# Mamba stage of a five-layer model: products of the late tiles issued beside those of the early tiles, and a section's first wait lowered by one copy

## The reference

```
B = (x @ W_B.T).reshape(b, L, h, n)          # h = 16 heads, n = 64 states
C = (x @ W_C.T).reshape(b, L, h, n)
X = x_in.reshape(b, L, h, p) * dt[..., None] # p = 8
Y_diag = einsum('bclhn,bcshn,bhcls,bcshp->bclhp', C, B, Lmat, X)
states = einsum('bclhn,bhcl,bclhp->bchpn', B, decay_states, X)
...
y = Y.reshape(b, L, d) * silu(z)
y = y @ W_out.T
```

## Time and profile before

| what | value |
|---|---|
| runs, us | 712.9, 714.73, 713.87; median 713.87 |
| profiled execution, us | 712.9, of which span 710.9 |
| granted TensorE clock, mean | 0.993 |
| share of the span busy: TensorE matmul, weight load | 94%, 70% |
| VectorE, ScalarE, GpSimd | 80%, 59%, 45% |
| sections of the Mamba stage | first D at 431.79 us, last O at 593.68 us |
| one section in the loop (516.91 to 537.42 us), granted clock | 1.00 |

### The profile page before, as it was taken

One profiled execution on the slowest core, in us unless ns is written; L12 is line 12 of the kernel. 1 busy time (PEld: TensorE's weight loads), 2 busy tenths in 40 slices (PEclk: granted clock), 3 DMA queues, 4 the chain that ended last, 5 costly groups with the idle time before them and its releaser, 6 DMA issues. The chain is left out here.

```text
span 710.9 us, 12357 instructions
## 1 busy us (share of the span) xinstructions
PE 665.9 (94%) x4084; PEld 498.0 (70%) x4084; DVE 566.6 (80%) x1303; ACT 416.6 (59%) x755; POOL 322.6 (45%) x403
## 2 busy tenths in 40 slices
PE   7899998797899999999999978999999998999997
PEld 5677774543457777777777767777777775777785
DVE  5789978989987888888989877666766676879775
ACT  4557685986335555556556567555656555555554
POOL 2568874101227756646647725220413300545463
PEclk8999999999999999999999999999999999999999
DMA  6625430000005232222222100000000000423241
GB/s 171 204 91 190 134 117 1 0 1 0 2 7 158 75 105 90 53 98 76 97 68 79 57 1 1 2 2 2 1 2 0 0 1 2 120 75 119 57 123 45
DMA packets 34345, 43.16 MB, mean 61 GB/s; under 512 B 5232, under 2 KB 17520, under 8 KB 34288
## 3 DMA queue, kind: packets, MB, share of 16 engines
q1 hardware_dynamic: 34288, 42.46, 19.6%
HBM read 41.13 MB, written 1.31 MB: 60 GB/s over the span
## 5 line engine op out<-in xcount | busy, mean ns | idle before, releaser
L726 POOL TENSOR_TENSOR p_prod<-p_p,p_gate_row 128x512 f32<-128x512 f32 x128 | 202.7, 1595 | 106.6 <-DVE p_p L524 59.6
L399 ACT ACTIVATE p_sil<-p_ps_a 128x512 f32<-128x512 f32 x176 | 105.1, 597 | 130.8 <-PE p_ps_a L100 125.0
L529 DVE TENSOR_TENSOR p_hlo<-p_prod,p_hhi 128x512 fp32r<-128x512 f32 x176 | 149.5, 851 | 0.3 <-ACT p_hhi L408 0.2
L524 DVE TENSOR_TENSOR p_p<-p_sil,p_ps_b 128x512 f32<-128x512 f32 x128 | 87.0, 680 | 51.9 <-ACT p_sil L399 36.1
L408 ACT CAST p_hhi<-p_prod 128x512 fp32r<-128x512 f32 x176 | 107.9, 614 | 23.1 <-POOL p_prod L726 23.1
L98 PE MATMUL p_ps_a<-xt_hi,w_uphi 128*128 128x512 f32 x176 | 74.3, 422 | 0.0
L98 PE MATMUL p_ps_acc<-p_hhi,w_downhi 128*128 128x512 f32 x176 | 71.1, 404 | 1.2 <-DVE p_hlo L529 1.0
L98 PE MATMUL p_ps_b<-xt_hi,w_uphi 128*128 128x512 f32 x176 | 70.8, 403 | 0.8 <-DVE p_prod L524 0.7
L99 PE MATMUL p_ps_a<-xt_lo,w_uphi 128*128 128x512 f32 x176 | 70.1, 398 | 0.0
L100 PE MATMUL p_ps_b<-xt_hi,w_uplo 128*128 128x512 f32 x176 | 70.0, 398 | 0.0
L100 PE MATMUL p_ps_a<-xt_hi,w_uplo 128*128 128x512 f32 x176 | 69.8, 397 | 0.0
(11 more groups left out here) (353 smaller groups left out, 1404.0 us busy)
## 6 DMA issues: line engine op xcount, KB each, us to landing
p_gate_row<-gate_rows SPq DMA_DIRECT2D x128, 256.0 KB, 3.3
w_rawbuf<-in_L_ffn_fc_w_dram SPq DMA_DIRECT2D x3, 512.0 KB, 6.8
w_rawbuf<-in_L_ffn_w_dram SPq DMA_DIRECT2D x3, 512.0 KB, 5.5
w_rawbuf<-in_L_ffn_shared_w_dram SPq DMA_DIRECT2D x3, 256.0 KB, 4.5
out_dram<-x SPq DMA_DIRECT2D x3, 256.0 KB, 3.7
x<-in_L_attn_x_dram SPq DMA_DIRECT2D x2, 256.0 KB, 3.7
x<-in_L_attn_x_dram SPq DMA_DIRECT2D x1, 512.0 KB, 9.0
mb_xraw<-in_L_attn_W_B_dram SPq DMA_DIRECT2D x1, 512.0 KB, 4.7
```

What stands on the lines that cost most here:

```text
L399: nc.scalar.activation(sil[:, u % 2], ps_a[:, u % 2], ACT.Silu).then_inc(c["sil"].sem, 1)
L524: nc.vector.tensor_tensor(dst, sil[:, u % 2], ps_b[:, u % 2], ALU.mult).then_inc(c["p1"].sem, 1)
L529: nc.vector.tensor_tensor(hlo[:, u % R], prod[:, u % R], hhi[:, u % R].bitcast(F32), ALU.subtract).then_inc(c["hlo"].sem, 1)
L726: G.tensor_tensor(prod[:, u % R], p1[:, u % 2], gate_row[:, e % ROWS], ALU.mult).then_inc(c["prod"].sem, 1)
```

## The change

A step's P1 now stands right behind P0, ahead of to_tokens and the outputs of the step before; D stays first. And P0 of a section's step 0 waits for three copies of B and C, not four. Nothing is added or left out.

```diff
@@ -1921,7 +1921,7 @@
             def bank_free(m, q, j, more):
 
                 if j == 0 and q == 0:
-                    pe.wait_ge(c["m_bh"].sem, c["m_bh"].at(m * 4 + 4))
+                    pe.wait_ge(c["m_bh"].sem, c["m_bh"].at(m * 4 + 3))
                     if m_positive(m):
                         pe.wait_ge(c["m_read"].sem, c["m_read"].at(m * 8))
                 elif j == 0:
@@ -1977,6 +1977,7 @@
                 for q in range(GROUPS):
                     decay(h, m, q)
                     products(h, m, q, 0, more)
+                    products(h, m, q, 1, more)
                     if q == 3 and not more:
                         tail.turn_y(pe, m - 1, ps_y)
                     if q == 1 and not first:
@@ -1988,7 +1989,6 @@
                         outputs(h, m, q - 1)
                     elif not first:
                         outputs(1 - h, m - 1, GROUPS - 1)
-                    products(h, m, q, 1, more)
                     if q == 0 and head is not None:
                         pe.wait_ge(c["m_out"].sem, c["m_out"].at(m - 1))
                         turn_head(head, ps_y)
```

## The result

The changed kernel took 710.88 us, median of 20 runs (708.09 to 713.0), against 713.5 us for the kernel before, also 20 runs (712.07 to 715.06). The ratio is 0.9963, 95% interval 0.9952 to 0.9974: faster by 0.37%, 2.6 us. The forecast was 709.8 in 707.8 to 712.4. The gain has the forecast's sign, and with 2.6 us it is two thirds of the 4.1 that I had summed up. That the time lies only 1.1 us from the forecast is in part luck: I had counted from the median of three runs, 713.87, and over 20 runs the kernel before stands at 713.5.

A forecast was written before the change was run, and what follows sets the result against it. A 3.22 us floor from D to piece, over the other engines, was taken to bound most steps; step gains summed to 3.95, taken as 4.1, off 713.87 us: 709.8, range 707.8 to 712.4.

The forecast's parts named there:

- The floor: Mamba steps: D, cap, exponential, copy, multiplication, piece take at least 3.22 us, so TensorE savings below that gain nothing.
- The sign that I had named: Profile after: some 20 of 28 pieces wait on VectorE's multiplication, about 7 us in total instead of 4.1.
- P1 beside P0: Same tile shape: P1 starts 0.86 us after P0, saving 0.20 in each of 31 steps on TensorE.
- O to the piece: TensorE's time from outputs to piece, not in the trace: taken as 0.79 us, between 0.64 and 1.06.
- The copy: Rival: P1 is held by ScalarE's copy of the piece before, only 2.0 us gained, 711.9 us; chance 0.20.
- late signal: Rival: P0's end signalled only after P1, copy off later than 1.88 after D, 3.9 us slower, 717.8; chance 0.06.
- The margin of 0.05: P1 may start 1.24 us after D, after the copy, and would be ready at 1.29: fits by 0.05.
- the bound by TensorE: Rival: TensorE bounds the stage, all 31 steps and the early P0s gain, 9.1 us less, 704.8; chance 0.10.
- The sum: Gains of all steps in the Mamba stage: 3.95 us, taken as 4.1 for section 7's earlier copy off.
- step 0 of sections 4 and 6: D to piece falls from 3.71 us to a floor of 3.24: 0.47 each, 0.9 together.
- Section 7: No pieces; VectorE and ScalarE set its pace; earlier P1 and P0 give 0.4 us, earlier copy off not counted.
- The step that failed: Stage behind the Mamba stage: starts with a barrier, unchanged, so the 4.1 us comes off the end.

The follow-up runs named there:

- extra_step1: Changed kernel with two of the late products' matmuls issued twice in step 1 of sections 0 to 6; stage 159.98 us, one run.
- order_only: Kernel before with only the order of products changed, a section's first wait staying at four copies; ratio 0.9977, stage 159.76 us.

## Why the prediction was right, and what was off

**The floor** was the right reading of the waits. All pieces of steps 1 to 3 in sections 1 to 6 start 3.22 to 3.24 after D, save the two that the masks hold up; extra work ahead of them cost nothing in steps 2 and 3, where I read room under the floor (in step 3 without any wait marked at the matmul), and its whole length in step 1 of sections 3 to 6, where I read none. Busy for 19.51 of 19.99 us of a section, TensorE was still not what set the distance from D to the piece in most steps. The sign that I had named was seen in part: I expected some 20 pieces waiting, about 7 us in total; the matmul row that I had counted by shows 7.9 us, but 13 pieces, and only the weight loads show 21, four of them doubtful.

**P1 beside P0**: 0.86 + 0.64 = 1.50 to the next shape was forecast, 1.51 measured. O to the piece was bounded between 0.64 and 1.06 and taken as 0.79. In section 4, step 1, 523.90 - 523.09 is 0.81; there the floor and TensorE's own time meet. In step 1 of extra_step1, where TensorE's own time is the later, it is 505.09 - 504.30 = 0.79.

**The copy and the late signal**: the copy of a piece held P1 in no step but the very first. P0 and P1 together are 1.58 us busy, and 1.67 in that one, where P0 no longer waits for copy 4 and P1 does. The margin of 0.05 was enough. The copy off stayed at 1.88. Both rivals that rested on these fall, and so does the bound by TensorE.

**The sum**: the stage gave 3.76 against 4.1. Step 1 of sections 3 to 6 0.74 (0.7 forecast), section 1 0.93 (0.95), section 2 0.51 (0.5), section 0 0.27 (0.3). Too high was step 0 of sections 4 and 6: D to piece 3.36 and 3.35, 0.7 together and not 0.9, because the floor in step 0 is 3.35, not the 3.24 that I allowed; section 3's the same, 0.1 instead of 0.2. Section 7 gave 0.57, for the 0.4 listed and the 0.15 rounded up on its account; whether by the copy off, as I had reasoned, was not separated. So the size that was off is the floor of step 0.

**The step that failed**, though the time came out in the range, is "the stage behind starts with a barrier and is not changed, so this comes off the end". Its code is unchanged and its time was not: in all four traces of the changed kernel the clock was at the lower level for its first 3 us, and the stretch from there to the end took about 0.8 us more than in the traces without such a drop. 713.5 - 3.76 + 0.8 = 710.5, against 710.88 measured. The later runs fit less well: there the changed kernel took 709.43 (7 runs) against 713.7, a gain of 4.3 us with the same drop in its trace. The time before the stage differs from run to run as well, so the medians don't show the 0.8 by themselves; the traces do. Of the 4.1, then, about 0.3 was a size that was off, and 0.8 a loss at a place that I had set to zero. Why the clock falls there stays open.

## What to carry to other kernels

Before pricing a saving on the busiest engine, measure in each step the distance from the event that feeds the other engines to the place where the busy engine has to wait for them; where several steps of different content show the same distance, a saving ahead of it is worth only what sticks out. Lifting such a floor helps only up to the next chain beside it, and that chain is found by asking what else each engine on it has queued ahead. And two edits that work in the same step should be priced together: here they gave 2.13 and 2.11 alone, and 3.76 together.

## What the runs showed of the hardware

Between traces of the same kernel the stage repeats to 0.05 us (158.13, 158.16, 158.18, 158.18), while the whole run moves by 5 us. Part of that is the granted clock: of the changed kernel's 20 runs the six with a mean clock of 0.988 took 711.2 to 713.0 us, the two at 0.998 took 708.09 and 709.25. A drop to the lower level behind the Mamba stage cost about 0.8 us and came in all four traces of the changed kernel and in neither of the kernel before, though TensorE was full again from the first matmul on. Ahead of that matmul it sat idle for 0.40, 0.78, 0.54 and 0.85 us within 5.4 us; the same four gaps in order_only brought no drop. A change of shape between groups costs TensorE about 0.2 us (P0 and P1 take 1.70 apart and 1.51 side by side); that it is the shape, and not something else in the change of group, was not varied by itself. The Trainium skill, TensorEngine Tiling (Array Packing), Key Properties, says that switching the mode drains the engine; by that rule a group behind one of its own shape saves the drain, and the trace agrees, with 0.19 us.
